# A gated cross-attention and low-rank expert layer: the first query pair is turned by blocks and DRAM instead of by TensorE, with another order in stage one and another boundary to stage two

## The chip, the cores and the metric
One core of a Trainium2 chip runs the whole kernel. The metric is the device time of one execution in microseconds (us); three runs of the kernel before gave a median of 930.25 us (928.26 to 930.46). The five engines are TensorE (PE in the profile; its weight loads are PEld), VectorE (DVE), ScalarE (ACT), GpSimd (POOL) and SyncE (SP, which only issues DMAs here). Each runs its own instructions in program order and waits on semaphores for the others.

## The reference
For each of 16 samples (x and ctx are 128 x 1024 float32), in short:
```python
qh = einsum('cn,oc->on', layernorm(x), Wq)  # 8 heads of 64 channels
kh = einsum('cn,oc->on', ctx, Wk); vh = einsum('cn,oc->on', ctx, Wv)
qh = softmax(qh, over the 64 channels of a head) * 64 ** -0.5
kh = softmax(kh, over the 1024 positions)
context = kh @ vh.T          # per head
out = context.T @ qh;  out = Wo @ out + bo
x = x + tanh(g_xattn) * out / norm(out, over channels) * g * sqrt(128)
y = layernorm(x)
scores = y @ Wr.T            # 64 experts, the top 16 are kept, softmax over them
x = x + tanh(g_ffn) * 2 * sum over k of gate[k] * (y @ A[k].T) @ B[k].T   # rank 16
```

## The kernel before
Every float32 product is made of three matmuls of rounded operands (`three_pass`, lines 59 to 63): each operand is split into a high half (a rounded copy) and a low half (what the rounding left). The high halves are mostly made by ScalarE, the low halves by VectorE or GpSimd.

**Stage one** (attention) is a software pipeline over the samples: `body(b)` of each engine works on keys and queries of sample b and finishes sample b-1, for b from 0 to 15, and a last body (16) has only the tail. TensorE multiplies keys in four blocks (`mm_k`) and queries in four pairs of position blocks (`mm_q(b, p)`, p from 0 to 3, two blocks of 128 positions and 512 channels each). VectorE takes the maxima (`max_k`, `max_q`), TensorE subtracts the query maxima (`shift_q`), ScalarE takes the exponentials (`exp_k`, `exp_q`), GpSimd adds halves of a head (`halve`), VectorE sums and inverts (`sum_q`), GpSimd scales (`normalise`). The queries then have to be turned: `tr_q` is eight TensorE transposes per pair into the PSUM tile `psT`, which has two banks shared by all transposes of keys and queries. ScalarE copies the high half from `psT` (`hi_q`), VectorE makes the low half (`lo_q`) and thereby frees the bank: `free_T` lets the next group of transposes wait for that.

Samples 1 to 14 ("turned" samples) already spare the transposes of their first key block: `exp_k(b, 0)` writes its result in an order of 32-column blocks, VectorE turns every 32x32 block in place (`turn_k`), SyncE writes the tile to DRAM and reads it back by strips (`move_k`, one DMA out and four in), ScalarE makes the high half (`hi_moved_k`) and GpSimd the low half (`lo_moved_k`).

`context` (24 matmuls, sample b-1) opens a body on TensorE, needs all low halves of the keys and gives `psX`, from which ScalarE makes `kc_hi` (`hi_kc`, line 709) and VectorE `kc_lo`; `fold` and `scale_m` make the matrix `mt`, `output` multiplies it by the turned queries, ScalarE adds the bias (`out_o`), and the result u goes to DRAM. In bodies 5 to 12 GpSimd also makes low halves of the expert weights A (`cast_a`, `lo_a`).

**The boundary.** In body 15 the work on stage two begins: the norms of samples 0 to 2 are spread over a tile (`spread` on VectorE, `spread_first`, `add_first` and `residual` on GpSimd) and added to x. SyncE loads x of sample 1 into `x_second` only when `spread_first(1)` is over (semaphore `u_done` at 2), since that tile lies over one that `spread_first(1)` reads.

**Stage two** (layer norm, routing, experts) is a loop `ffn_body`, b from 1 to 15: `up` multiplies by A in three pieces, `down(b-1)` by B. The chain of one sample is long: `sum_u` (TensorE) and `norm_u` (VectorE) give the norm, `residual` (GpSimd) x plus attention, `stats2` (VectorE) mean and deviation, `normalise` (ScalarE) y, `turn_y`, `move_y` (sixteen ScalarE copies of 32x256) and `hi_moved_y`/`lo_moved_y` turn y for `up`; `route`, `gated`, `turn_h`, `move_h`, `hi_moved_h`/`lo_moved_h` do the same for `down`.

The order of all this is written out by hand; there is no scheduler.

Of the kernel before, what the change touches and what calls it, by code (L numbers as in the profile page):

```python
# [1731 lines left out]
```

## Time and profile before
| | us |
|---|---|
| median of 3 runs | 930.25 |
| the profiled execution, its own time | 932.08 |
| its span | 930.4 |
| TensorE busy | 901.6 (97%) |
| VectorE busy | 739.7 (80%) |
| ScalarE busy | 684.3 (74%) |
| GpSimd busy | 520.0 (56%) |

The profile is of one execution. Busy time of TensorE is modelled from pipelined matmuls, so it does not show the engine at its peak, and what counts are the waits between its instructions. GpSimd's 56% is a mean over two stages: it is nearly idle in stage two.

### The profile page before, as it was taken

What the parts mean: (1) busy time and instruction counts of PE and PEld (TensorE: products, weight loads), DVE (VectorE), ACT (ScalarE), POOL (GpSimd) and SP (SyncE); (2) the same over time, 40 slices, a digit from 0 to 9 for tenths busy, and PEclk for the clock granted to TensorE, in tenths of its full rate; (3) what the DMA queues carried; (4) which work ended last, traced back from release to release, by engine and by line L of the source; (5) the groups of instructions that cost most, each with busy time, mean ns of one, the idle gap of its engine ahead of it and who ended that gap; (6) DMA issues with size and microseconds to landing.
All of it is one profiled execution on the core that took longest, in us unless ns stands there. A gap on an engine that the chain in (4) does not pass through costs nothing.

```text
span 930.4 us, 15943 instructions
## 1 busy us (share of the span) xinstructions
PE 901.6 (97%) x4732; PEld 764.7 (82%) x4732; DVE 739.7 (80%) x1523; ACT 684.3 (74%) x1400; POOL 520.0 (56%) x342
## 2 busy tenths in 40 slices
PE   7899999999999999999999999969999999999998
PEld 5687888878787787888887798869999999999896
DVE  6888889988888898898887778777777777777642
ACT  4787787777778777876876758687888888888731
POOL 3686778789778878977789856221222222222200
PEclk9999999999999999999999999979999999999999
DMA  4323423452453444233322784111111211111001
GB/s 158 114 91 125 173 103 124 161 173 100 161 182 106 146 137 159 90 137 135 119 89 87 230 329 154 46 68 68 69 69 68 69 68 68 68 68 68 23 24 46
DMA packets 35319, 104.04 MB, mean 112 GB/s; under 512 B 4432, under 2 KB 11600, under 8 KB 35280
## 3 DMA queue, kind: packets, MB, share of 16 engines
q1 hardware_dynamic: 29520, 82.59, 25.2%
q0 software_dynamic: 5472, 20.45, 6.9%
q10 hardware_dynamic: 288, 0.52, 0.2%
q8 instruction: 19, 0.31, 0.1%
q14 instruction: 20, 0.16, 0.1%
HBM read 79.43 MB, written 24.12 MB: 111 GB/s over the span
## 4 chain that ended last, share of the span: by engine, by line
PE 63%; DVE 9%; POOL 8%; issue 8%; ACT 7%; DMA 2%; SPq 0%; POOLq 0%; ACTq 0%; DVEq 0%
PE ps L61 19%; PE ps L63 18%; PE ps L62 18%; PE ps L1455 3%; PE ps L1464 3%; POOL qe L451 2%; ACT h_raw L776 2%; ACT qe L683 2%; POOL ctx_lo L410 2%; PE ps L1445 1%; DMA turn_scratch<-ek 1%; POOL qhalf L444 1%; POOL aT_lo L464 1%; ACT qT_hi L691 1%; DVE qmax L1002 1%
## 5 line engine op out<-in xcount | busy, mean ns | idle before, releaser
L522 POOL TENSOR_TENSOR rb<-u_in,rb 128x1024 f32<-128x1024 f32 x14 | 33.7, 2409 | 224.7 <-DVE rb L992 224.7
L451 POOL TENSOR_TENSOR qe<-qe,qrec 128x1024 f32<-128x1024 f32 x64 | 121.3, 1906 | 16.3 <-DVE qrec L1010 16.3
L61 PE MATMUL ps<-aT_hi,yT_hi 128*128 128x448 f32 (+2 forms) x360 | 121.1, 337 | 3.7 <-DVE yT_lo L1154 3.7
L62 PE MATMUL ps<-aT_hi,yT_lo 128*128 128x448 f32 (+2 forms) x360 | 119.7, 332 | 0.0
L63 PE MATMUL ps<-aT_lo,yT_hi 128*128 128x448 f32 (+2 forms) x360 | 119.4, 332 | 0.0
L776 ACT ACTIVATE h_raw<-hg 32x256 f32<-32x256 f32 x248 | 103.0, 415 | 16.8 <-DVE hg L1159 14.0
L444 POOL TENSOR_TENSOR qhalf<-qe 128x512 f32<-128x512 f32 x64 | 82.3, 1286 | 57.8 <-ACT qe L683 55.9
L1016 DVE TENSOR_TENSOR qT_lo<-ps,qT_hi 128x512 fp32r<-128x512 f32 x128 | 81.5, 679 | 34.7 <-ACT qT_hi L691 34.2
L776 ACT ACTIVATE y_raw<-u_in 32x256 f32<-32x256 f32 x224 | 92.9, 415 | 4.8 <-DVE u_in L1150 2.4
L61 PE MATMUL ps<-bT_hi,hT_hi 128*128 128x512 f32 x240 | 93.7, 390 | 0.3 <-DVE hT_lo L1172 0.3
L62 PE MATMUL ps<-bT_hi,hT_lo 128*128 128x512 f32 x240 | 93.5, 390 | 0.0
L63 PE MATMUL ps<-bT_lo,hT_hi 128*128 128x512 f32 x240 | 93.4, 389 | 0.0
L676 ACT ACTIVATE qe<-ps 128x1024 f32<-128x1024 f32 x48 | 49.6, 1033 | 52.9 <-PE ps L1445 52.7
L996 DVE TENSOR_REDUCE kmax<-ps 128x1 f32<-128x1024 f32 x64 | 78.0, 1219 | 10.5 <-PE ps L63 8.3
L691 ACT ACTIVATE qT_hi<-ps 128x512 fp32r<-128x512 f32 x128 | 69.5, 598 | 14.0 <-PE ps L1464 14.0
L61 PEld LDWEIGHTS ps<-aT_hi,yT_hi 128*128 128x128 f32 x360 | 69.2, 192 | 6.7 <-DVE yT_lo L1154 4.1
L668 ACT ACTIVATE ek<-ps,kmax 128x1024 f32<-128x1024 f32 x64 | 72.1, 1127 | 3.0 <-DVE kmax L996 3.0
L698 ACT ACTIVATE ekT_hi<-ps 128x512 fp32r<-128x512 f32 x100 | 54.8, 605 | 22.1 <-PE ps L1455 21.5
L62 PEld LDWEIGHTS ps<-aT_hi,yT_lo 128*128 128x128 f32 x360 | 69.3, 192 | 2.2
L63 PEld LDWEIGHTS ps<-aT_lo,yT_hi 128*128 128x128 f32 x360 | 69.1, 192 | 1.9
L1464 PE MATMUL ps<-ident,qe 128*128 128x128 f32 x512 | 67.2, 274 | 1.5 <-DVE ekT_lo L1027 1.5
L1464 PEld LDWEIGHTS ps<-ident,qe 128*128 128x128 f32 x512 | 59.2, 140 | 10.7 <-POOL qe L451 1.4
(179 smaller groups left out, 2558.8 us busy)
## 6 DMA issues: line engine op xcount, KB each, us to landing
x_in<-in_x SPq DMA_DIRECT2D x16, 512.0 KB, 3.3
ctx_in<-in_ctx SPq DMA_DIRECT2D x16, 512.0 KB, 5.4
ctxT_in<-in_ctxT SPq DMA_DIRECT2D x16, 512.0 KB, 3.3
ctxT_hi<-in_ctxT POOLq DMA_DIRECT2D x16, 512.0 KB, 4.1
u_scratch<-osb SPq DMA_DIRECT2D x16, 512.0 KB, 3.0
x<-in_x SPq DMA_DIRECT2D x15, 512.0 KB, 3.8
out<-res SPq DMA_DIRECT2D x15, 512.0 KB, 2.9
turn_scratch<-ek SPq DMA_DIRECT2D x14, 512.0 KB, 4.3
```

The lines of the kernel that those rows point to most:

```text
L61: nc.tensor.matmul(psum, whi, mhi, start=start, stop=False)
L62: nc.tensor.matmul(psum, wlo, mhi, start=False, stop=False)
L63: return nc.tensor.matmul(psum, whi, mlo, start=False, stop=stop)
L444: nc.gpsimd.tensor_tensor(qhalf[:, p % 2, :].rearrange("p (h d) -> p h d", d=DH // 2), v[:, :, 0:DH // 2], v[:, :, DH // 2:DH], ALU.add).t ...
L451: nc.gpsimd.tensor_tensor(v, v, w, ALU.mult).then_inc(q_norm, 1)
L668: nc.scalar.activation(to, of, ACT.Exp, bias=kmax[:, j:j + 1], accum_out=ksum[:, j:j + 1]).then_inc(k_exp, 1)
L691: nc.scalar.activation(qT[0][:, :, n * P:n * P + P], psT[:, h, :].rearrange("p (j n) -> p j n", n=P), ACT.Copy).then_inc(q_hi, 1)
L698: nc.scalar.activation(ekT[0][:, 4 * h:4 * h + 4, j * P:j * P + P], psT[:, h, :].rearrange("p (n d) -> p n d", d=P), ACT.Copy).then_inc(k_ ...
L776: last = nc.scalar.activation(dst[32 * q:32 * q + 32, 256 * a:256 * a + 256], src[32 * a:32 * a + 32, 256 * q:256 * q + 256], ACT.Copy)
L996: nc.vector.tensor_reduce(kmax[:, j:j + 1], psK, axis=AX.XY, op=ALU.max, negate=True).then_inc(k_max, 1)
L1016: nc.vector.tensor_tensor(qT[1][:, :, v], psT[:, h, :].rearrange("p (j n) -> p j n", n=P), qT[0][:, :, v].bitcast(f32), ALU.subtract).then ...
L1464: last = nc.tensor.transpose(psT[:, h, j * P:j * P + P], qe[:, p, w:w + P], ident[:, :])
```

## The change
Three things change together.

1. The first query pair of every sample (p = 0) is no longer transposed by TensorE. `exp_q(b, 0)` writes in 32-column blocks, `halve` and `normalise` of that pair follow that layout (the latter in two instructions), VectorE turns the blocks (`turn_q`), SyncE moves them through DRAM (`move_q`, one DMA out and four in, back into the same tile `qe`), ScalarE makes the high half in two instructions (`hi_q(b-1, 0)`, in the next body) and GpSimd the low half in two (`lo_moved_q`).
2. The order of stage one changes on all engines: on VectorE `lo_q(b-1, 1)` comes before `scale_m`, and six steps of the deviation of the next sample come after `sum_q(b, 0)`; on TensorE `shift_q(b, 1)` comes before the first half of `output`; on GpSimd `lo_a` moves to the head of the next body; on ScalarE `hi_q(b-1, 1)` comes before `exp_k(b, 1)` and `hi_moved_k` after `exp_q(b, 1)`.
3. At the boundary VectorE's `spread(1)` and GpSimd's `spread_first(1)` move to the end of body 15, and in the first bodies of stage two the norms of samples 3 and 4, the statistics of sample 3 and the routing are taken in another order; ScalarE's `square_u(4)` is split to fit, and TensorE takes `sum_u(3)` a piece earlier and `sum_u(5)` a piece later.

```diff
+        def moved_q(h):
+
+            return qe[:, 0, :].rearrange("p (a m i) -> p m a i", a=P // 32, i=32)[:, CH * h:CH * h + CH]
+
+        def turned_q(tile, h):
+
+            return tile[:, :, P * h:P * h + P].rearrange("p m (a i) -> p m a i", i=32)
...
+def move_q(b):
+
+    wait_apart(sp, sp_turns, (q_turned, b + 1))
+    sp.dma_start(turn_q_dram, qe[:, 0, :]).then_inc(q_put, 16)
+    wait_apart(sp, sp_turns, (q_put, PUT * (b + 1)))
+    for q in range(P // 32):
+        sp.dma_start(qe[32 * q:32 * q + 32, 0, :].rearrange("j (a f) -> j a f", f=256),
+                     turn_q_dram.rearrange("(a j) (q f) -> q j a f", a=P // 32, f=256)[q]).then_inc(q_moved, 16)
...
             load(x_in[:, :], x, b + 2, x_loaded)
+    if head:
+        move_q(b)
+    if ahead:
         wait_apart(sp, sp_turns, (c_lo, b + 1))
         load(ctxT_in[:, :], ctxT, b + 1, ctxT_loaded)
     if tail:
...
+    if p == 0:
+        v = qe[:, 0, :].rearrange("p (s r n i) -> p s r n i", s=2, r=2, i=32)
+        nc.gpsimd.tensor_tensor(qhalf[:, 0, :].rearrange("p (n s i) -> p s n i", s=2, i=32),
+                                v[:, :, 0], v[:, :, 1], ALU.add).then_inc(q_half, 1)
+        return
     v = qe[:, p, :].rearrange("p (h d) -> p h d", d=DH)
     nc.gpsimd.tensor_tensor(qhalf[:, p % 2, :].rearrange("p (h d) -> p h d", d=DH // 2),
                             v[:, :, 0:DH // 2], v[:, :, DH // 2:DH], ALU.add).then_inc(q_half, 1)
 
 def normalise(b, p):
     pool.wait_ge(q_rec, 4 * b + p + 1)
+    if p == 0:
+        for s in range(2):
+            v = qe[:, 0, s * HD:s * HD + HD].rearrange("p (r n i) -> p r n i", r=2, i=32)
+            w = qrec[:, 0, :].rearrange("p (n s) -> p s n", s=2)[:, s, :]
+            w = w.unsqueeze(1).unsqueeze(3).broadcast_to([P, 2, 2 * CH, 32])
+            last = nc.gpsimd.tensor_tensor(v, v, w, ALU.mult)
+        last.then_inc(q_norm, 1)
+        return
     v = qe[:, p, :].rearrange("p (h d) -> p h d", d=DH)
     w = qrec[:, p, :].unsqueeze(2).broadcast_to([P, 2 * H, DH])
     nc.gpsimd.tensor_tensor(v, v, w, ALU.mult).then_inc(q_norm, 1)
+
+def lo_moved_q(b):
+    for h in range(2):
+        pool.wait_ge(q_hi, 8 * b + h + 1)
+        nc.gpsimd.tensor_tensor(turned_q(qT[1], h), moved_q(h), turned_q(qT[0], h).bitcast(f32),
+                                ALU.subtract).then_inc(q_moved_lo, 1)
...
-def body(b, head, tail, ahead, split=False):
-    if split:
+def body(b, head, tail, ahead, low=False, cast=False):
+    if low:
+        lo_a(b - SPLIT - 1)
+    if cast:
         cast_a(b - SPLIT)
     if tail:
         halve(b - 1, 3)
-    if head:
+    if head and not started(b):
         lo_xn(b, 1)
     if tail:
+        lo_moved_q(b - 1)
         normalise(b - 1, 2)
+    if head:
+        halve(b, 0)
+    if tail:
         normalise(b - 1, 3)
-    if head:
-        halve(b, 0)
-    if head and not ahead:
-        spread_first(0)
     if tail:
         pool.wait_ge(m_hi, b)
         nc.gpsimd.tensor_tensor(mts[1][:, :, :], mt[:, :, :], mts[0][:, :, :].bitcast(f32),
                                 ALU.subtract).then_inc(m_lo, 1)
-    if split:
-        lo_a(b - SPLIT)
-    if head and turned(b):
-        lo_moved_k(b)
+    if head and started(b):
+        lo_xn(b, 1)
     if head and not ahead:
-        add_first(0)
+        spread_first(0)
     if head:
         normalise(b, 0)
         hi_c(b)
+        if turned(b):
+            lo_moved_k(b)
     if head and not ahead:
         for t in range(3):
             hi_a(t)
+        add_first(0)
     if ahead:
         lo_ctx(b + 1, 0)
         lo_ctx(b + 1, 1)
     if head:
         halve(b, 1)
         lo_c(b)
-    if head and not ahead:
-        spread_first(1)
     if head:
...
     if head and not ahead:
+        spread_first(1)
         add_first(1)
...
-        act.wait_ge(q_T, 8 * b + 2 * p - 6)
+    if started(b) and p == 0:
+        act.wait_ge(q_moved_lo, 2 * b)
+    elif started(b):
+        act.wait_ge(q_T, 6 * b - 6 + 2 * p)
...
+        act.wait_ge(q_moved, MOVED * (b + 1))
+        for h in range(2):
+            nc.scalar.activation(turned_q(qT[0], h), moved_q(h), ACT.Copy).then_inc(q_hi, 1)
+        return
...
     if tail:
+        hi_q(b - 1, 0)
         hi_kc(b - 1)
...
         exp_q(b, 0)
+        if tail:
+            hi_q(b - 1, 1)
         exp_k(b, 1)
     if tail:
-        if head:
-            hi_q(b - 1, 1)
         hi_m(b - 1)
         if not head:
...
     if head and turned(b):
-        hi_moved_k(b)
         hi_q(b - 1, 2)
     elif head:
         hi_k(b, 0)
     if head:
         exp_k(b, 2)
         exp_q(b, 1)
+    if head and turned(b):
+        hi_moved_k(b)
     if tail and head and not turned(b):
         hi_q(b - 1, 2)
     if ahead:
...
+def turn_q(b):
+    dve.wait_ge(q_norm, 4 * b + 1)
+    nc.vector.transpose(qe[:, 0, :], qe[:, 0, :]).then_inc(q_turned, 1)
...
-    if tail and head:
+    if tail and ahead:
         sum_q(b - 1, 3)
...
         max_k(b, 1)
     if last:
+        sum_q(b - 1, 3)
+    if last:
         dve.wait_ge(ctx_lo, 2 * NB)
         spread(0, rb_first[0], n_newton, 4 * NEWTON)
-    if ahead and started(b):
-        std(b + 1, range(3, NCH + 1))
     if tail and not head:
         lo_y(0)
         lo_q(b - 1, 1)
+    if tail and head:
+        lo_q(b - 1, 1)
     if tail:
         scale_m(b - 1)
-    if tail and head:
-        lo_q(b - 1, 1)
     if tail and not head:
         stats2(1, 1)
         lo_q(b - 1, 2)
-    if head and turned(b):
-        max_k(b, 2)
-        max_q(b, 1)
-    elif head:
+    if head:
         max_q(b, 1)
         max_k(b, 2)
+    if head and not turned(b):
         lo_k(b, 0)
     if not started(b):
         std(b + 1, range(5, NCH + 1))
     if head:
         sum_q(b, 0)
+    if ahead and started(b):
+        std(b + 1, range(3, NCH + 1))
     if tail and head:
         lo_q(b - 1, 2)
-    if last:
-        dve.wait_ge(xn_lo, 2 * NB)
-        spread(1, rb_first[1], n_newton, 4 * NEWTON)
     if head:
         max_k(b, 3)
         max_q(b, 2)
+        turn_q(b)
         lo_k(b, 1)
...
         std2(0, range(4, NCH + 1))
-    if head:
-        lo_q(b, 0)
+        dve.wait_ge(xn_lo, 2 * NB)
+        spread(1, rb_first[1], n_newton, 4 * NEWTON)
...
+norm_steps(3, range(7))
...
     if first:
         lo_moved_h(0)
         turn_y(2, 0)
+        norm_steps(3, range(7, NRT))
         for n in range(3, TOP):
             route_step(1, n)
+        spread_u(3)
     elif second:
+        result(0, 0, 0, 0)
+        part_u(4)
+        for n in range(3):
+            route_step(2, n)
+        lo_moved_h(1)
         turn_y(3, 1)
-        route(2)
         norm_u(4)
+        for n in range(3, TOP):
+            route_step(2, n)
     else:
         result(b - 2, (j + 1) % 2, (j + 3) % SLOTS, 2 * i + (j - 1) // 2)
+        if third:
+            part_u(5)
         lo_moved_h(b - 1)
-        if norms:
+        if norms and not third:
             part_u(b + 2)
         if ahead:
             turn_y(b + 1, j % 2)
...
             norm_u(b + 2)
     for p in range(len(PIECES)):
         gated(b, p)
+    if first:
+        lo_moved_y(2)
     turn_h(b)
-    if ahead:
+    if ahead and not first:
         lo_moved_y(b + 1)
-    if first:
-        norm_u(3)
-        result(0, 0, 0, 0)
-        part_u(4)
-        lo_moved_h(1)
...
+    if head and turned(b):
+        shift_q(b, 1)
     if tail and head:
         output(b - 1, 0, range(CH // 2))
-    if head:
+    if head and not turned(b):
...
     if head:
-        tr_q(b, 0, next(turn))
         shift_q(b, 3)
...
-    late = isinstance(i, int) and b <= 2
+    late = isinstance(i, int) and 2 <= b <= 3
```

VectorE in a body of stage one, from the last maxima before the turn to the low halves after it. Before (`kmax` and `qmax` are `max_k(b, 3)` and `max_q(b, 2)`, `ekT_lo` is `lo_k(b, 1)`, `qT_lo` is `lo_q`):
```order
L1044 TENSOR_TENSOR mt<-ps,krec 64x512 x2
L1014 ISA
L1016 TENSOR_TENSOR qT_lo<-ps,qT_hi 128x4x128
...
L996 TENSOR_REDUCE kmax<-ps 128x1
L1002 TENSOR_REDUCE qmax<-ps 128x16
L1025 ISA
L1027 TENSOR_TENSOR ekT_lo<-ps,ekT_hi 128x4x128
```
And now:
```order
L1082 TENSOR_TENSOR qT_lo<-ps,qT_hi 128x4x128
L1110 TENSOR_TENSOR mt<-ps,krec 64x512 x2
...
L1058 TENSOR_REDUCE kmax<-ps 128x1
L1064 TENSOR_REDUCE qmax<-ps 128x16
L1076 STREAM_TRANSPOSE qe<-qe 128x1024
L1091 ISA
L1093 TENSOR_TENSOR ekT_lo<-ps,ekT_hi 128x4x128
```
`lo_q(b-1, 1)` moved ahead of `scale_m` (`mt`), and the turn of the query pair stands between the maxima and `lo_k(b, 1)`.

SyncE from the loads at the boundary on. Before (`x_second` is x of sample 1, the next store is `store_u(14)`):
```order
L281 DMA x_0_105<-in_x 128x1024
L281 DMA u_first<-u_scratch 128x1024
L281 DMA x_second<-in_x 128x1024
L285 DMA u_scratch<-osb 128x1024
L281 DMA u_in_103<-u_scratch 128x1024
```
And now:
```order
L291 DMA x_0_105<-in_x 128x1024
L291 DMA u_first<-u_scratch 128x1024
L291 DMA x_second<-in_x 128x1024
L329 DMA turn_q_scratch<-qe 128x1024
L332 DMA qe<-turn_q_scratch 32x4x256 x4
L295 DMA u_scratch<-osb 128x1024
```
The move of the last sample's query pair stands behind the load of `x_second`.

GpSimd at the same place, now (`qhalf` is `halve(15, 2)`, then `spread_first(1)`, `add_first(1)`, `halve(15, 3)`):
```order
L513 DMA aT_hi<-in_AT 128x1088 x5
L471 TENSOR_TENSOR qhalf<-qe 128x512
L547 TENSOR_TENSOR u_first<-u_first,rb_first_101 128x1024
L557 TENSOR_TENSOR x_1_106<-x_second,u_first 128x1024
L471 TENSOR_TENSOR qhalf<-qe 128x512
```
Before, `spread_first(1)` stood between `lo_c(15)` and `normalise(15, 1)`, ahead of the five casts of A.

## Rows read from the trace of the kernel before

**Rows 1.** The page's first line.
```profile
span 930.4 us, 15943 instructions
```

**Rows 2.** Timeline of ScalarE (start, length, engine, line, operation): `hi_kc`, one per sample.
```profile
44.88 0.60 ACT L709 ACTIVATE kc_hi<-ps 128x512 fp32r<-128x512 f32 x1 [1.07 <-PE ps L63]
...
498.16 0.60 ACT L709 ACTIVATE kc_hi<-ps 128x512 fp32r<-128x512 f32 x1
...
533.40 0.60 ACT L709 ACTIVATE kc_hi<-ps 128x512 fp32r<-128x512 f32 x1 [0.17 <-PE ps L63]
```

**Rows 3.** Timeline of TensorE's weight loads, one sample of stage one.
```profile
353.45 1.01 PEld L1464 LDWEIGHTS ps<-ident,qe 128*128 128x128 f32 x8
...
355.71 0.19 PEld L61 LDWEIGHTS ps<-ctx_hi,wk_hi 128*128 128x128 f32 x1 [0.70 <-POOL ctx_lo L410]
...
362.21 1.02 PEld L1464 LDWEIGHTS ps<-ident,qe 128*128 128x128 f32 x8
363.49 0.19 PEld L61 LDWEIGHTS ps<-ekT_hi,ctxT_hi 128*128 128x128 f32 x1 [0.26 <-ACT osb L726]
```

**Rows 4.** Timeline of VectorE, the same sample.
```profile
333.37 1.19 DVE L1021 STREAM_TRANSPOSE ek<-ek 128x1024 f32<-128x1024 f32 x1
...
340.62 0.27 DVE L82 TENSOR_SCALAR std_t<-rstd,std_h 128x1 f32<-128x1 f32 x1
...
342.44 1.41 DVE L1044 TENSOR_TENSOR mt<-ps,krec 64x512 f32<-64x512 f32 x2
...
351.17 1.23 DVE L1002 TENSOR_REDUCE qmax<-ps 128x16 fp32r<-128x1024 f32 x1 [0.22 <-PE ps L63]
352.32 1.28 DVE L1027 TENSOR_TENSOR ekT_lo<-ps,ekT_hi 128x512 fp32r<-128x512 f32 x2
...
361.47 1.28 DVE L1027 TENSOR_TENSOR ekT_lo<-ps,ekT_hi 128x512 fp32r<-128x512 f32 x2
```

**Rows 5.** Timeline of ScalarE, the same sample.
```profile
340.19 1.03 ACT L676 ACTIVATE qe<-ps 128x1024 f32<-128x1024 f32 x1 [2.84 <-PE ps L1445]
...
342.20 1.09 ACT L691 ACTIVATE qT_hi<-ps 128x512 fp32r<-128x512 f32 x2
```

**Rows 6.** Busy time by stretch: PE, PEld, DVE, ACT, POOL, clock, DMA share, GB/s.
```profile
343.50:376.00 32.50, 32.16 (x172) 26.11 (x171) 28.10 (x49) 24.55 (x51) 27.01 (x18) 1.00 0.38 130
```

**Rows 7.** Groups by form: a low half by GpSimd from SBUF in blocks of 32.
```profile
L436 POOL TENSOR_TENSOR ekT_lo<-osb,ekT_hi 128x1024 fp32r<-128x1024 f32 x14 | 33.5, 2396 | 0.0
```

**Rows 8.** Timeline of SyncE at the end of stage one.
```profile
522.35 0.33 SPq L281 DMA_DIRECT2D x_second<-in_x  x1
```

**Rows 9.** Timeline of GpSimd, the same stretch.
```profile
519.94 2.38 POOL L506 TENSOR_TENSOR u_first<-u_first,rb_first 128x1024 f32<-128x1024 f32 x1
```

**Rows 10.** Timeline of VectorE, the same stretch.
```profile
528.45 0.21 DVE L1073 TENSOR_SCALAR nb<-mv,y 128x1 f32<-128x1 f32 x1
```

**Rows 11.** Chain that ended last (start, length, what): the key's way through DRAM.
```profile
269.52 6.39 DMA turn_scratch<-ek
277.32 2.87 DMA osb<-turn_scratch
```

**Rows 12.** The page's DMA issues: the key tile's way out (KB, us to landing).
```profile
turn_scratch<-ek SPq DMA_DIRECT2D x14, 512.0 KB, 4.3
```

**Rows 13.** Timeline of TensorE's matmuls at the start of stage two.
```profile
607.66 0.74 PE L61 MATMUL ps<-aT_hi,yT_hi 128*128 128x448 f32 x1 [3.67 <-DVE yT_lo L1154]
...
618.94 0.64 PE L1520 MATMUL ps<-part,sel 128*128 128x32 f32 x2 [4.62 <-DVE part L1190]
...
619.86 0.52 PE L62 MATMUL ps<-aT_hi,yT_lo 128*128 128x384 f32 x1
...
624.34 0.45 PE L61 MATMUL ps<-aT_hi,yT_hi 128*128 128x384 f32 x1
...
625.87 0.33 PE L63 MATMUL ps<-aT_lo,yT_hi 128*128 128x384 f32 x1
```

**Rows 14.** Timeline of ScalarE, the same stretch.
```profile
594.58 1.24 ACT L761 ACTIVATE u_in<-x,nb,y 128x1024 f32<-128x1024 f32 x1 [5.31 <-DVE nb L1073]
```

More of the change, by code:

```diff
@@ L589, in _ @@
             pool.sem_inc(a_low, 1)
-            with pool.Fori(SPLIT, SPLIT + DC) as b:
-                body(b, head=True, tail=True, ahead=True, split=True)
-            with pool.Fori(SPLIT + DC, NB - 2) as b:
-                body(b, head=True, tail=True, ahead=True)
+            body(SPLIT, head=True, tail=True, ahead=True, cast=True)
+            with pool.Fori(SPLIT + 1, SPLIT + DC) as b:
+                body(b, head=True, tail=True, ahead=True, low=True, cast=True)
+            body(SPLIT + DC, head=True, tail=True, ahead=True, low=True)
             body(NB - 2, head=True, tail=True, ahead=True)
@@ L884, in body @@
                     out_o(b - 1, 1, early)
-                if head:
-                    hi_q(b, 0)
                 if head and not ahead:
@@ L910, in ffn_body @@
                 hi_moved_h(b - 1)
+                if isinstance(i, int) and b == 2:
+                    exp_scores(2)
                 if not isinstance(i, int) or b <= NB - 2:
                     normalise(b + 1, (j + 2) % SLOTS)
-                exp_scores(b)
+                if isinstance(i, int) and b == 2:
+                    square_u(4, 0, 2, (1,))
+                else:
+                    exp_scores(b)
                 if not isinstance(i, int) or b <= NB - 2:
@@ L916, in ffn_body @@
                     hi_moved_y(b + 1)
+                if isinstance(i, int) and b == 1:
+                    square_u(4, 0, 2, (0,))
                 move_h(b)
-                if not isinstance(i, int) or b <= NB - 4:
+                if not isinstance(i, int) or 2 <= b <= NB - 4:
                     square_u(b + 3, j % 2, 2 * i + (j + 4) // 2)
@@ L1191, in part_u, with norm_steps, spread_u @@
                                         op=ALU.add, apply_transpose=True).then_inc(n_part, 1)
-            def norm_u(e):
-                before = NRT * (e - EARLY)
-                for k in range(NRT):
-                    norm_step(k, e - EARLY + 2, psN.unsqueeze(1), 1, before)
-                dve.wait_ge(x2_done, e)
-                spread(0, rb, n_step, before + NRT)
+            def norm_steps(e, steps):
+                for k in steps:
+                    norm_step(k, e - EARLY + 2, psN.unsqueeze(1), 1, NRT * (e - EARLY))
+            def spread_u(e):
+                dve.wait_ge(x2_done, e)
+                spread(0, rb, n_step, NRT * (e - EARLY + 1))
+            def norm_u(e):
+                norm_steps(e, range(NRT))
+                spread_u(e)
             stats(0)
@@ L1332, in _ @@
             turn_h(0)
+            part_u(EARLY)
             lo_b(0)
             lo_b(1)
-            part_u(EARLY)
             std2(2, range(NCH + 1))
@@ L1346, in ffn_body @@
                 second = isinstance(i, int) and b == 2
+                third = isinstance(i, int) and b == 3
                 if first:
@@ L1543, in up @@
                 elif p == 2:
[L1544 removed]
+                    pe.wait_ge(q_lo, 6 * NB)
                 first, width = PIECES[p]
@@ L1576, in body @@
                          + [("k", b, 0)] * (head and not turned(b)) + [("q", b - 1, 2)] * tail + [("k", b, 1)] * head
-                         + [("q", b - 1, 3)] * tail + [("k", b, 2), ("k", b, 3), ("q", b, 0)] * head)
-                first = ("q", b - 1, 0) if tail else None
+                         + [("q", b - 1, 3)] * tail + [("k", b, 2), ("k", b, 3)] * head)
+                first = ("k", b - 1, 3) if tail else None
                 turn = iter([first] + order[:-1])
@@ L1631, in body @@
                 if tail and head:
-                    output(b - 1, 0, range(CH // 2, CH))
+                    output(b - 1, 0, range(CH // 2, CH if ahead else CH - 1))
                 if head:
@@ L1636, in body @@
                     tr_q(b - 1, 3, next(turn))
+                if tail and not ahead:
+                    output(b - 1, 0, range(CH - 1, CH))
                 if ahead:
```

42 lines of the change are left out of this document (25 added, 17 removed).

## The prediction
> **What bounds the kernel now.** I read the page's first line [rows 1] and the table of busy times first. TensorE is busy for 97% of the span, so a microsecond counts only if TensorE's own work shrinks or one of its waits does. Then I took ScalarE's timeline for the marker `hi_kc`, one per sample, directly behind `context` [rows 2]: fourteen periods lie between 44.88 and 498.16, so a turned body lasts 453.28 / 14 = 32.38 us, and the last body with a head lasts 35.24 us. Then I read one turned body on TensorE's weight loads, on VectorE and on ScalarE [rows 3 to 5], its busy times [rows 6] and the price of the like of the new low half [rows 7], the end of stage one and the way through DRAM [rows 8 to 12], and the start of stage two [rows 13, 14]. The reader is to see three things. Inside a body TensorE hardly waits: the largest wait is 0.70 us, for GpSimd's `ctx_lo`. VectorE works in one unbroken train from 342.44 to 353.60, with stops of 0.2 to 0.3 us. At the start of stage two TensorE stands still for 3.67 and 4.62 us, and after each wait it runs at the lower of its two clock levels.
>
> **Part 1: eight transposes less.** The group `tr_q(b, 0)` loads from 362.21, and the next `context` from 363.49 [rows 3], a price of 1.28 us per body. All of it would be gain if nothing else were late. But `context` also needs `lo_k(b, 3)`, which ends at 361.47 + 1.28 = 362.75 [rows 4]. Without the transposes `context` can start at 362.8 at the earliest, so 0.7 us can be had, not 1.28.
>
> **Part 2: what VectorE gets in its place.** Per body it loses two halves of `lo_q(b, 0)`, 1.2 us that stood where it had time, and gains `turn_q`, a transpose of the form of `turn_k`, which takes 1.19 us and blocks the engine for 1.11 [rows 4]. It is put in the train, ahead of `lo_k(b, 1)`, and this is the step on which my forecast rests. I lay out the new train in the times of the body shown. `exp_q(b, 0)` starts at 340.19 as before, since nothing ahead of it changes; ScalarE is free at about 341.15 for `hi_q(b-1, 1)`, whose two halves took 1.09 us together [rows 5], so its first half is ready at about 341.75. VectorE is free at 340.62 [rows 4]; before, it used this time for six steps of the deviation and `nbias`, 342.44 - 340.62 = 1.82 us. Now `lo_q(b-1, 1)` is next and it idles till 341.8, and the 1.82 us come later, inside the train. From there everything is queued back to back, for the inputs are ready in time. The train before took 353.60 - 342.44 = 11.16 us, with some 0.55 us of short stops, so 10.6 us of work. Now it is 341.8 + 10.6 + 1.82 + 1.11 = 355.3 when `lo_k(b, 1)` ends, against 353.60.
>
> Who waits for it: `tr_q(b-1, 3)` uses the banks that `lo_k(b, 1)` frees, one half after the other. TensorE reached it at 353.45 [rows 3], and VectorE ended 0.15 us after that, with the second half needed only 0.5 us later; so the cover was some 0.4 us. Now the first half can start at 354.7 and the second at 355.35; the group ends at 355.9 instead of 354.5. Queued behind it are `mm_k(b+1, 0)`, `tr_k(b, 2)`, half an `output`, `mm_q(b, 3)` and `tr_k(b, 3)`. The wait of 0.70 us for `ctx_lo` before 355.71 [rows 3] is then covered. So `mm_k(b+1, 0)` (1.36 us) ends at 357.2 instead of 356.3, everything up to `lo_k(b, 3)` is 0.9 us later, and the next `context` starts at 362.75 + 0.9 + 0.05 = 363.7 against 363.49. The 0.7 us of part 1 are eaten, and the body takes 32.52 + 0.2 = 32.7 us. The same chain holds in bodies that were shorter before, because it goes by VectorE and not by what GpSimd did. Fourteen bodies: 14 x (32.7 - 32.38) = **+4.5 us**. The ends for a body are 31.2 (the train has slack I don't see, and only the end of `lo_k(b, 3)` counts: 32.38 - 0.7 and the wait for `ctx_lo` gone, 0.5) and 33.0. Last body with a head: the transposes go, and the stop at the turn comes in: **-1.2 us**.
>
> **Part 3: GpSimd.** It is busy for 27.01 of 32.50 us in a body with `lo_a` [rows 6]. `lo_moved_q` adds two instructions of 128 x 512 in blocks of 32; the like of 128 x 1024 took 2.40 us [rows 7], so 2.4 to 2.6 us, and `normalise(b, 0)` in two perhaps 0.1. That makes 29.7 of 32.7 us. `lo_a` moves into the wait for `exp_q(b-1, 3)` at the body's head, so what stands before `ctx_lo` grows and shrinks by the same 2.5 us. I cost it at nothing; if the cover were gone, each body would have GpSimd's 30 us and its two waits of 1 to 2 us as its length, which is the upper end of 33.0. The move through DRAM takes 6.39 us out and 2.87 us back in its slow case [rows 11]. It starts after `turn_q` at about 354.2 and is back at 364, and `hi_q` asks for it about 4 us after that: hidden.
>
> **Part 4: the last sample's move.** Here the same way is not hidden. SyncE issues in order, and `move_q(15)` stands behind the load of `x_second`, which waits for `spread_first(1)`. Before, that was over by 519.94 + 2.4 and the load was issued at 522.35 [rows 8, 9]. Now its `spread(1)` is VectorE's last work in body 15: after the last `nbias` of the statistics at 528.45 [rows 10], so 528.6 to 529.8; `spread_first(1)` runs from 530.0 to 532.4. SyncE issues `x_second` (0.33) and then the DMA out at about 532.8. With 4.3 us (the median for the key tile [rows 12]) to 6.39 us out and 2.87 us back [rows 11] plus the issues, the pair lands at 540.5 to 543. On ScalarE `hi_q(15, 0)` stands ahead of `hi_kc(15)`: `kc_hi` at 541.8 instead of 533.40 [rows 2], and behind it wait `lo_kc`, `fold` and, all of TensorE. **+8.2 us** (6 to 11). After such a wait the clock is low again: the fifteen matmuls from 619.86 to 624.34 stood 0.32 us apart, the eight after them 0.19 [rows 13], 2 us lost; **+2.0 us**. The Trainium skill ("TensorE: Matmul & The Clock Gate", What's actually happening) says that the array's clock goes between 1.2 and 2.4 GHz with recent activity, which agrees with these two spacings; without that rule the sum would be 2 us lower.
>
> **Part 5: stage two.** TensorE waited 3.67 us for y of sample 3 [rows 13], because `stats2(3)` came last in the first body and ScalarE sat 5.31 us until `nb` [rows 14]. Now the norm of sample 3 is ready before, `residual(3)` follows, and `nb` is some 6 us earlier: by the same chain (`normalise` 1.2, `turn_y` 1.2, sixteen copies 6.8, high 1.1, low 1.2) y is there at about the time that TensorE asks. The wait of 4.62 us for the partial sums of sample 5 goes because `sum_u(5)` is asked for 4 us later and `part_u(5)` comes before `lo_moved_h(2)`. The two waits are 8.3 us and the low clock behind them cost 2.2 after the second (above) and by my estimate 1.5 after the shorter first. What is late next: `lo_moved_y(2)` now stands behind `spread_u(3)` and beside GpSimd's `residual(3)`, 0.8 us, and `sum_u(4)`, `y(3)` half a microsecond each; I leave 2 us. **-10.0 us** (-5 to -12).
>
> **Sum.** The span was 930.4 and the execution 932.08, 1.8 above the median of 930.25. 4.5 - 1.2 + 8.2 + 2.0 - 10.0 = +3.5: a span of 933.9, an execution of 935.6, and 933.8 beside the median.
>
> **The rivals.**
> A. *TensorE stays the bound in stage one.* If the train has room (stops that I take for work, or `max_k(b, 3)` early enough), a body falls to 31.2 us: -16.5 instead of +4.5, so 912.8. For it speaks that VectorE is busy only 80%; against it, the gapless train of rows 4 and a cover of 0.4 us.
> B. *The last move is not waited for*, since the load of `x_second` is passed earlier than I think. Then parts of 8.2 and 2.0 fall away: 923.6. Against it: the order of SyncE and GpSimd shown with the change.
> C. *Stage two keeps its waits* in another place, since eleven steps of the norm, `result` and `part_u` are only shuffled on an engine that is nearly full there. Then -10 becomes -1: 942.8, slower. It decides where `y(3)` comes more than 3 us after 604.
> D. *The change's gain is as drawn*: A and B at once, 902.6.
>
> **How the numbers follow.** Forecast 0.56, A 0.16, B 0.14, C 0.10, D 0.04. A measurement of this kernel tells 0.3%, that is 2.8 us, from no change. The forecast's own range is 928 to 939; within it faster 0.05, same 0.20, slower 0.31, since 933.8 lies just over the line of 933.0. A, B and D are faster (0.34), C is slower. Together faster 0.39, same 0.20, slower 0.41. The range of eight in ten is 912 to 942: it takes in A and B and leaves out D and most of C.
>
> **What would show it.** Right: VectorE without a gap from about 11 us after the start of `context` to the end of `lo_k(b, 1)` 24.3 us after it; TensorE idle for 1.2 us before `tr_q(b-1, 3)`, released by `ekT_lo`; `hi_kc` 32.7 us apart; the last `hi_kc` 8 us late behind a DMA of `qe`, with a low clock after it; no wait over 1 us where stage two begins. Wrong: `hi_kc` closer than 32 us (A), `fold(15)` less than 2 us after its transposes (B), a wait over 3 us for `yT_lo` or `part` (C).

## The result, and the profile after

| | before | changed | forecast |
|---|---|---|---|
| median (lowest to highest), us | 930.36 (928.26 to 930.64) | 954.03 (952.59 to 956.08) | 933.8 (912 to 942) |
| ratio, 95% interval | | 1.0261 [1.0237, 1.0285] | |

The change makes the kernel 2.6% slower, and the time lies 12 us above my range. The profiled execution has a span of 952.3 us against 930.4 [rows 1]. The profiled execution before was itself 1.8 us above its median, and this one is at its median, so differences of spans below can come out up to 1.8 us smaller than those of medians.

The marker `hi_kc` of [rows 2] on ScalarE, with the row ahead of the last one:

```profile
44.23 0.60 ACT L762 ACTIVATE kc_hi<-ps 128x512 fp32r<-128x512 f32 x1 [1.90 <-PE ps L63]
...
501.48 0.72 ACT L762 ACTIVATE kc_hi<-ps 128x512 fp32r<-128x512 f32 x1
...
546.59 1.15 ACT L739 ACTIVATE qT_hi<-qe 128x512 fp32r<-128x512 f32 x2 [10.30 <-DMA qe<-turn_q_scratch]
547.64 0.58 ACT L762 ACTIVATE kc_hi<-ps 128x512 fp32r<-128x512 f32 x1
```

Cut at these markers, the 21.9 us by which the span grew are:

| stretch | before | changed | difference | forecast |
|---|---|---|---|---|
| start to first `hi_kc` | 44.88 | 44.23 | -0.7 | 0 |
| fourteen bodies | 453.28 | 457.25 | +4.0 | +4.5 |
| last body with a head | 35.24 | 46.16 | +10.9 | +7.0 (8.2 - 1.2) |
| last `hi_kc` to the end | 397.0 | 404.7 | +7.7 | -8.0 (2.0 - 10.0) |

The fourteen bodies went as drawn. The last line is the failure: 15.7 us of the error of 18.4 in the span. TensorE's waits from 530 us on (engine, tile, line, who released it: us in total, times, longest), which answer to [rows 13]:

```profile
PE ps L61 <- DVE kc_lo L1098: 10.6, 1, 10.6
PE ps L61 <- DVE hT_lo L1238: 8.4, 1, 8.4
PE ps L1601 <- DVE part L1256: 4.9, 1, 4.9
PE ps L61 <- DVE ekT_lo L1093: 0.9, 1, 0.9
PE ps L1613 <- ACT qe L731: 0.3, 1, 0.3
PE ps L61 <- DVE yT_lo L1220: 0.3, 1, 0.3
```

The wait for y of sample 3, 3.67 us before, is 0.3. The wait for `part` is still there, one body later (at 663.14, for `sum_u(6)`). A wait of 8.4 us for `hT_lo` (the low half that `lo_moved_h(0)` makes) before `down(0)` is new. VectorE's timeline says where it comes from:

```profile
583.10 0.18 DVE L1031 TENSOR_SCALAR ns<-ps 128x32 f32<-128x32 f32 x1
583.32 1.58 DVE L67 TENSOR_SCALAR nr<-ns 128x32 int32<-128x32 int32 x1
584.93 2.27 DVE L1035 TENSOR_TENSOR nt<-nr,ns 128x32 f32<-128x32 f32 x1
587.23 2.26 DVE L1037 SCALAR_TENSOR_TENSOR nt<-nt,nr 128x32 f32<-128x32 f32 x1
589.52 2.27 DVE L1039 SCALAR_TENSOR_TENSOR nr<-nt,nr 128x32 f32<-128x32 f32 x1
591.82 0.19 DVE L1035 TENSOR_TENSOR nt<-nr,ns 128x32 f32<-128x32 f32 x1
592.05 0.19 DVE L1037 SCALAR_TENSOR_TENSOR nt<-nt,nr 128x32 f32<-128x32 f32 x1
592.16 1.22 DVE L1238 TENSOR_TENSOR hT_lo<-h_raw,hT_hi 128x1024 fp32r<-128x1024 f32 x1
```

These are the seven norm steps that the change puts ahead of `lo_moved_h(0)`. Four of them take 1.58 to 2.27 us and three 0.18 or 0.19, for the same 32 columns. The busy time hides the cause, because these rows are counted as work. GpSimd's timeline beside them:

```profile
575.94 15.80 POOL L522 TENSOR_TENSOR bT_lo<-b_raw,bT_hi 128x1024 fp32r<-128x1024 f32 x6 [1.94 <-DMA bT_hi<-in_BT]
```

It ends at 591.74, and from 591.82 the steps are short. While it runs, the four long steps take about one GpSimd instruction each (15.80 / 6 = 2.6 us).

### The profile page after: what moved, and what is told of

Read it like the earlier page. It is cut to its first block, busy times and chain, and to the rows that moved or that the text cites. A ratio compares the mean times of both kernels' runs of the same rounds, so it can differ in the third digit from the quotient of the medians.

```text
span 952.3 us, 15772 instructions
## 1 busy us (share of the span) xinstructions
PE 892.8 (94%) x4604; PEld 751.7 (79%) x4604; DVE 746.4 (78%) x1507; ACT 684.3 (72%) x1400; POOL 563.2 (59%) x390
## 4 chain that ended last, share of the span: by engine, by line
PE 55%; DVE 22%; issue 9%; ACT 6%; POOL 4%; DMA 2%; DVEq 0%; ACTq 0%; SPq 0%; POOLq 0%
PE ps L61 17%; PE ps L62 17%; PE ps L63 17%; DVE qmax L1064 3%; DVE ekT_lo L1093 3%; DVE kmax L1058 3%; DVE qT_lo L1082 2%; ACT h_raw L831 2%; PE ps L1544 2%; PE ps L1535 1%; DVE mt L1110 1%; DVE std_t L82 1%; DVE qsum L1069 1%; DVE rstd L84 1%; PE ps L1525 1%
## 5 line engine op out<-in xcount | busy, mean ns | idle before, releaser
L486 POOL TENSOR_TENSOR qe<-qe,qrec 128x1024 f32<-128x1024 f32 x48 | 91.4, 1905 | 10.7 <-DVE qrec L1072 10.7
L1082 DVE TENSOR_TENSOR qT_lo<-ps,qT_hi 128x512 fp32r<-128x512 f32 x96 | 61.5, 682 | 26.7 <-ACT qT_hi L744 26.7
L744 ACT ACTIVATE qT_hi<-ps 128x512 fp32r<-128x512 f32 x96 | 53.5, 598 | 30.6 <-PE ps L1544 30.6
L471 POOL TENSOR_TENSOR qhalf<-qe 128x512 f32<-128x512 f32 x48 | 61.8, 1288 | 19.9 <-ACT qe L731 19.7
L1544 PE MATMUL ps<-ident,qe 128*128 128x128 f32 x384 | 52.7, 277 | 14.2 <-DVE ekT_lo L1093 14.2
L751 ACT ACTIVATE ekT_hi<-ps 128x512 fp32r<-128x512 f32 x100 | 54.4, 601 | 15.8 <-PE ps L1535 15.8
L1544 PEld LDWEIGHTS ps<-ident,qe 128*128 128x128 f32 x384 | 43.3, 140 | 26.3 <-DVE ekT_lo L1093 17.7
```

The source lines that it names most:

```text
L471: nc.gpsimd.tensor_tensor(qhalf[:, p % 2, :].rearrange("p (h d) -> p h d", d=DH // 2), v[:, :, 0:DH // 2], v[:, :, DH // 2:DH], ALU.add).t ...
L744: nc.scalar.activation(qT[0][:, :, n * P:n * P + P], psT[:, h, :].rearrange("p (j n) -> p j n", n=P), ACT.Copy).then_inc(q_hi, 1)
L751: nc.scalar.activation(ekT[0][:, 4 * h:4 * h + 4, j * P:j * P + P], psT[:, h, :].rearrange("p (n d) -> p n d", d=P), ACT.Copy).then_inc(k_ ...
L1082: nc.vector.tensor_tensor(qT[1][:, :, v], psT[:, h, :].rearrange("p (j n) -> p j n", n=P), qT[0][:, :, v].bitcast(f32), ALU.subtract).then ...
L1544: last = nc.tensor.transpose(psT[:, h, j * P:j * P + P], qe[:, p, w:w + P], ident[:, :])
```

## The experiments

Every kernel is the changed one with one edit, unless it says otherwise. The kernel before took 931.3, 929.8 and 930.5 us beside the three groups of four in which they ran (`move_first`, `hlo_first`, `turn_behind`, `old_stage_two`; `spread_early`, `spread_move`, `pool_waits`, `turn_std`; the other four). The changed kernel was not run again with them, so a gain against its 954.03 us carries an uncertainty of about 1 us.

**1. The last move first.** On SyncE:

```diff
+            move_q(NB - 1)
             sp.wait_ge(u_done, 2)
             load(x_second[:, :], x, 1, xr_loaded[1])
-            body(NB - 1, head=True, tail=True, ahead=False)
+            body(NB - 1, head=False, tail=True, ahead=False)
```

> SyncE issues the last query pair's move (to DRAM and back) before it waits for u_done 2 and loads x_second; nothing else changes against the changed kernel. Theory 1 (queue order): in the changed kernel DVE had turned the pair at 520.2 us but SyncE stood at the wait until 535.46, so with the move first it is through by about 530, the fold is released by ACT alone and the last kc_hi comes near 537.5 instead of 547.64; PE's 10.6 us wait falls to 1 to 3 us and the clock is not lowered there. 954.0 becomes 943 (941 to 945). Rival (the DRAM trip itself is slow in this stretch because weights are being loaded): the trip still lands near 545 and the time stays at 952 to 954.

Measured 950.24 us, 1.0200 [1.0183, 1.0217]. `hi_kc(15)` comes at 538.43 and the fold waits 0.98 us, as the theory says, but only 3.8 us of the expected 11 arrive, since another wait takes over. The first matmul of `up(0, 0)`, and on GpSimd the wait that it goes back to:

```profile
549.01 0.74 PE L61 MATMUL ps<-aT_hi,yT_hi 128*128 128x448 f32 x1 [7.52 <-DVE yT_lo L1212]
```

```profile
533.47 2.41 POOL L548 TENSOR_TENSOR u_first<-u_first,rb_first 128x1024 f32<-128x1024 f32 x1 [0.37 <-DVE rb_first L1055]
543.26 2.34 POOL L558 TENSOR_TENSOR x<-x_second,u_first 128x1024 f32<-128x1024 f32 x1 [7.39 <-DMA x_second<-in_x]
```

`spread_first(1)` is as late as before the edit, so `x_second` is asked for at 535.90, and `add_first(1)` holds up GpSimd. `halve(15, 3)` stands behind it, and VectorE, which has `sum_q(15, 3)` ahead of `lo_y(0)`, waits for that:

```profile
546.84 0.69 DVE L1070 TENSOR_REDUCE qsum<-qhalf 128x16 f32<-128x512 f32 x1 [7.11 <-POOL qhalf L472]
```

I had named `spread_first(1)` in my prediction as what SyncE waits for, and had not followed it to `add_first(1)`.

**2. The spread early again**, as in the kernel before; then this and edit 1 together. The same lines are taken out at their later places:

```diff
+                if last:                                 # VectorE, ahead of max_k(b, 3)
+                    dve.wait_ge(xn_lo, 2 * NB)
+                    spread(1, rb_first[1], n_newton, 4 * NEWTON)
...
                     lo_c(b)                              # GpSimd
+                if head and not ahead:
+                    spread_first(1)
```

> spread_first(1) on GpSimd and the spread of rb_first1 on VectorE stand again where the kernel before has them (behind lo_c(15) and ahead of max_k(15,3)); nothing else changes against the changed kernel. With the move alone put first, the fold's wait of 10.6 us fell to 1.0 but a wait of 7.5 us for yT_lo came, since x_second was loaded from 535.90 and GpSimd's add_first(1) and what stands behind it waited for it until 543.26. Theory 1b (the late spread_first(1) is the cause of both): u_done 2 comes near 526, x_second and the move go out at 526 and are in by 534 and 538, the last kc_hi comes at about 538 instead of 547.64 and no wait for yT_lo follows; with the 1.4 us of low clock gone 954.0 becomes 943 (941 to 945). Rival (DRAM trips in this stretch are slow, 7 us out and 5 back, whoever issues them when): kc_hi near 542 and 946 to 949.

> The same as spread_early, and SyncE moves the last query pair before it waits for u_done 2. Theory 1b: the move is hidden altogether (in by 536), kc_hi near 537.5 behind ACT's last exponentials, x_second is issued at 529 and in by 537, so yT_lo comes just in time: 942 to 943, at most 1 us below spread_early. Rival (x_second is what counts): slower than spread_early by 2 to 4, with a wait for yT_lo before up(0,0).

Measured 951.4 us, 1.0229 [1.0212, 1.0246], and 942.14 us, 1.0130 [1.0113, 1.0147]. Alone it gives 2.6, with the move first 11.9. The first kernel lies outside both ranges: `hi_kc(15)` comes only at 545.26, later even than its rival put it. DRAM trips are slow in this kernel, but not whoever issues them when, as the rival has it; the second kernel's are not. What each DMA of the way back took to land, in `spread_early`, then in the changed kernel:

```profile
L332 SPq DMA_DIRECT2D qe<-turn_q_scratch x4: 326/459/731, 532.8 to 534.4; - x4
...
DMA to landing us min/median/max: 7.5/7.7/9.8
```

```profile
L332 SPq DMA_DIRECT2D qe<-turn_q_scratch x4: 326/425/432, 542.4 to 543.7; - x4
...
DMA to landing us min/median/max: 2.5/2.8/2.9
```

And the busy share of the DMA engines in `spread_early` (last column but one):

```profile
524.00:528.00 4.00, 4.00 (x25) 3.43 (x24) 3.75 (x12) 2.03 (x5) 4.00 (x3) 1.00 0.01 3
528.00:532.00 4.00, 3.12 (x15) 2.28 (x14) 3.82 (x10) 1.69 (x3) 4.00 (x7) 1.00 0.98 297
532.00:536.00 4.00, 4.00 (x20) 3.24 (x18) 0.96 (x3) 3.95 (x16) 3.27 (x2) 1.00 1.08 375
536.00:540.00 4.00, 2.27 (x18) 1.73 (x16) 0.00 (x0) 0.56 (x3) 1.28 (x1) 1.00 1.06 338
```

GpSimd issues five loads of `aT_hi`, 544 KB each, from 528.9 on. What SyncE issues from 532.8 is behind them in time. It does not wait for `x_second`, which landed 4.2 us after its issue at 527.12, before the way back was asked for. In `move_first` the way back went out from 528.46, when the loads began (529.04), and its four DMAs took 2.6 to 7.6 us. In `spread_move` it goes out from 527.08, ahead of them, takes 2.6 to 3.2 us, and TensorE hardly waits: 0.2 us before the fold and 0.3 for `yT_lo`. So two causes cover one another, the order on SyncE and the late `spread_first(1)`: alone each edit shows a third of what the two give together, or less. That the burst of weights is the third is read from these traces; no run moves the loads.

**3. `hT_lo` ahead of the seven steps:**

```diff
-            norm_steps(3, range(7))
...
                     lo_moved_h(0)
                     turn_y(2, 0)
-                    norm_steps(3, range(7, NRT))
+                    norm_steps(3, range(NRT))
```

> The seven first steps of norm_steps(3) stand behind lo_moved_h(0) and turn_y(2,0) instead of ahead of them; nothing else changes against the changed kernel. Theory 2 (the seven small steps wait one by one for GpSimd's bT_lo instructions, and hT_lo stands behind them): hT_lo starts at about 583 and takes one GpSimd instruction more than its 1.2 us (2.4 us), down(0) starts at about 585.7 instead of 593.43 with no low clock in it; a wait of 2 to 3 us for yT_lo before up(2) comes in its place since gated(1) is late, so the time falls by 6 to 8: 947 (945 to 949). Rival (hT_lo is late because of ACT or of memory traffic): down(0) stays near 593 and the time stays within 2 us of 954.

Measured 949.46 us, 1.0190 [1.0173, 1.0207], so -4.6 where -7 was expected, and 0.5 above the range. `down(0)` starts at 586.19 after a wait of 1.0 us; `hT_lo` takes 2.83. But the steps still stand beside GpSimd, `gated(1)` and `lo_moved_y(2)` behind them are late, and 4.39 us of wait for `yT_lo` come before `up(2, 0)`, where I expected 2 to 3.

**4. GpSimd waits for the steps:**

```diff
+            pool.wait_ge(n_step, 7)
             for k in range(KC):
                 if by_pool(k):
                     lo_b(k)
```

> GpSimd waits for the seventh step of norm_steps(3) before its first bT_lo instruction; nothing else changes against the changed kernel. Theory 2 (a VectorE instruction with both inputs in SBUF waits for the end of GpSimd's running tensor_tensor): with GpSimd idle all seven steps take 0.15 to 0.25 us each, lo_b(0) and lo_b(1) take 1.2 us each instead of 4.53 for the two, hT_lo is ready 3 us or more before PE's down(0) could start; down(0) starts near 584 instead of 593.43 but waits inside for bT_lo (GpSimd works from about 580 on, six by 2.5 us), and ends near 600 instead of 606.7: 947 (944 to 951). Rival (the steps are slow for another reason, such as waits between neighbours): they still take 2.3 us each.

Measured 951.0 us, 1.0223 [1.0206, 1.0240], the upper end of the range expected. The time is 3.0 lower, not 7, since `down(0)` then waits for `bT_lo` inside (3.0 us in three waits), but the question was the length of the steps. VectorE here:

```profile
580.79 0.18 DVE L67 TENSOR_SCALAR nr<-ns 128x32 int32<-128x32 int32 x1
581.01 0.19 DVE L1036 TENSOR_TENSOR nt<-nr,ns 128x32 f32<-128x32 f32 x1
581.24 0.19 DVE L1038 SCALAR_TENSOR_TENSOR nt<-nt,nr 128x32 f32<-128x32 f32 x1
581.47 0.19 DVE L1040 SCALAR_TENSOR_TENSOR nr<-nt,nr 128x32 f32<-128x32 f32 x1
...
582.47 3.21 DVE L1239 TENSOR_TENSOR hT_lo<-h_raw,hT_hi 128x1024 fp32r<-128x1024 f32 x1 [0.36 <-ACT hT_hi L858]
```

The same four instructions, 0.18 to 0.19 us each with GpSimd idle. GpSimd starts at 582.20, and now `hT_lo` pays, 3.21 us for work of 1.22. This shows that the steps are long because GpSimd's instructions run beside them. The Trainium skill ("SBUF — State Buffer", SBUF: two separate sides) says that GpSimd and some VectorE operations, those with two inputs in SBUF among them, share one port pair that whoever starts first holds for its whole instruction; the trace agrees, with 2.27 us for an instruction of 0.19.

**5. The second stage by itself**, from both sides: the changed kernel with the second stage of the kernel before (`ffn_body` of VectorE and ScalarE, VectorE's lines ahead of it and TensorE's `late`), and the kernel before with that of the changed one, of which these are the core:

```diff
-                late = isinstance(i, int) and b <= 2
+                late = isinstance(i, int) and 2 <= b <= 3
...
+            norm_steps(3, range(7))
```

> Stage one and the boundary as in the changed kernel, the second stage in the order of the kernel before. From the last kc_hi (547.64) to the end the kernel before took 397.0 us, the changed one 404.7. Theory 2 (the new order of stage two costs 8 by itself): 547.6 + 397 + 1.5 for the low clock at the start = 946.5 (944 to 949), with hT_lo blocked once (2.4 us) and no wait of 8 us before down(0). Rival (stage two is slow because of what stage one leaves it, GpSimd being later against VectorE): down(0) waits 5 us or more with the old order too, and the time is 951 to 956.

> The kernel before with the changed kernel's order of the second stage and nothing else of the change. Theory 2 (the seven norm steps wait for GpSimd's bT_lo one by one and hold hT_lo): down(0) waits 7 to 9 us for hT_lo, the wait of 3.67 us for yT_lo goes, the one of 4.6 us for part stands one body later, and the time from the last kc_hi to the end is 402 to 405 us instead of 397.0: 936 to 939 beside about 930. The prediction's reading (the new order takes both waits away): 920 to 925.

Measured 946.32 us, 1.0161 [1.0144, 1.0178], as theory 2 put it, and 936.48 us, 1.0059 [1.0044, 1.0073], the low end of what it put. From the last `hi_kc` the first takes 943.6 - 546.45 = 397.1 us, the second 934.8 - 533.18 = 401.6. So the old order takes 397 us behind either stage one, and the new one costs 4.6 us of span behind the old stage one (6.0 by the medians) and 7.6 behind the new one. TensorE's waits in the kernel before with only this part:

```profile
PE ps L61 <- DVE hT_lo L1181: 8.5, 1, 8.5
PE ps L1545 <- DVE part L1199: 4.2, 1, 4.2
```

**6. The turn behind `lo_k(b, 1)`**, and then also the last std steps where the kernel before has them:

```diff
-                    turn_q(b)
                     lo_k(b, 1)
+                    turn_q(b)
```

> DVE turns the query pair behind lo_k(b,1) instead of ahead of it; nothing else changes against the changed kernel. Theory 3 (the row of VectorE work ahead of lo_k(b,1) is what lengthens a body): lo_k(b,1) is 1.1 us earlier, the waits of 0.92 and 1.25 us for ekT_lo before tr_q(b-1,3) go, the turn fills an idle stretch of 0.8, and a body is 0.7 to 1.0 us shorter: 31.8 instead of 32.66, 954.0 becomes 942 (940 to 945). Rival (the body is bound by TensorE or by another chain, the waits come back elsewhere): body within 0.2 of 32.66, 951 to 955.

> turn_q behind lo_k(b,1) as in turn_behind (942.7, body 31.95 us), and besides the last std steps (1.8 us) stand where the kernel before has them, ahead of lo_q(b-1,1), where VectorE idles 1.04 us for qT_hi. Theory 3: PE was busy 438.6 of 446.5 us in turn_behind, so at most 0.5 us a body is left; the steps fill the idle stretch and lo_k(b,1) comes 1 us earlier still: body 31.6 to 31.9, time 938 to 942. Rival (mt is now late, by 0.8 us, and the fold and m chain with it): body 32.0 to 32.3, 943 to 948.

Measured 942.74 us, 1.0120 [1.0103, 1.0137], and 951.02 us, 1.0236 [1.0213, 1.0259]. Bodies last (491.74 - 44.49) / 14 = 31.95 us and (498.75 - 43.71) / 14 = 32.50. One line moved by one place gives 11.3 us. The second kernel's body lies above its rival's 32.3, and its time, 3 us above the rival's range: all waits for `ekT_lo` ahead of `tr_q(b-1, 3)` are gone there too, but `lo_q(b-1, 1)`, `mt` and `qmax` of `max_q(b, 1)` stand behind the std steps, `shift_q(b, 1)` starts 0.4 us later in the body, and the `output` behind it 0.5:

```profile
346.01 0.70 PE L1525 MATMUL ps<-qmax,ident_r 128*128 128x512 f32 x2 [0.17 <-DVE qmax L1064]
```

The stretch in which VectorE idles 1.04 us was not free to fill: what it waits for there is on TensorE's path as well.

**7. `sum_u` behind `up(b, 1)` in every body from 2 on:**

```diff
-                late = isinstance(i, int) and 2 <= b <= 3
+                late = not isinstance(i, int) or b >= 2
```

> sum_u stands behind up(b,1) in every body from b = 2 on, not only in 2 and 3; nothing else changes against the changed kernel. Theory 4 (the wait of 4.95 us for part belongs to the first body whose sum stands ahead of up(b,1), while usq of that body is made behind move_h; in the bodies of the loop the sum has 4 us more anyway): the wait at 663 goes, nothing replaces it, 954.0 becomes 947.5 to 950 (the low clock after it goes too). Rival (it only moves to the next body or comes back as a wait for hg or yT_lo): 952 to 955.

Measured 946.19 us, 1.0169 [1.0154, 1.0183]; 1.3 us below the range expected. The wait of 4.95 us is 0.64, nothing takes its place, and the granted clock behind it is 1.00 (662 to 667 us), where it was 0.50 in the changed kernel (663 to 668).

**8. All of it together:** edits 1 and 2, the turn behind `lo_k(b, 1)` and the old stage two; then `late = True` besides.

> The turn of the query pair with its three costs taken away: turn_q behind lo_k(b,1); spread_first(1) and its spread as in the kernel before with the last move put first on SyncE; the second stage in the order of the kernel before. By the profiles of the single edits: kc_hi of body 14 at 491.7 (turn_behind), 37.2 to the last one (spread_move), 397.1 to the end (old_stage_two), 1.7 around: 927.7 (925 to 930) beside 930.4 for the kernel before, a ratio of 0.997. Rival (the gains overlap or the turn pays nothing against the kernel before): 930 to 935.

> best_turn, and sum_u behind up(b,1) in every body. By theory 4 the wait of 3.7 us for part goes with the low clock behind it: 4 to 6 us below best_turn, 922 to 924. Rival (the wait comes back elsewhere): within 1 us of best_turn.

Measured 925.39 us, 0.9950 [0.9938, 0.9962], and 919.97 us, 0.9884 [0.9869, 0.9898]. Both beat the kernel before, by 0.5% and 1.2%. The second is 2 us below the range expected, since the first was already 2 below the middle of its own; the 5.4 between them are as expected. The bodies of the first last (491.01 - 43.77) / 14 = 31.95 us against 32.38 before, so the turned query pair is worth 6 us once nothing else pays for it. TensorE's largest waits after 500 us in the faster one:

```profile
PE ps L61 <- DVE yT_lo L1215: 3.8, 1, 3.8
PE ps L1512 <- DVE qmax L1059: 1.2, 1, 1.2
```

## Why the prediction was wrong

Part 5 failed. I wrote that in stage two both waits go with their low clocks, and left 2 us for what is late next: -10.0. By itself the part costs +4.6 (experiment 5), since a new wait of 8.4 us for `hT_lo` comes in and the wait for `part` stays. With the stop at the boundary ahead of it the stretch costs 7.7, of which 1.4 lie before `turn_h(0)`, where I had put 2.0 of low clock (the granted clock is 0.50 from 549.0 to 553.5).

- The first half was wrong, though the 3.67 us for `yT_lo` went. I had `nb` of sample 3 some 6 us earlier. Before and now:

```profile
594.33 0.22 DVE L1073 TENSOR_SCALAR nb<-mv,y 128x1 f32<-128x1 f32 x1
```

```profile
609.75 0.21 DVE L1139 TENSOR_SCALAR nb<-mv,y 128x1 f32<-128x1 f32 x1
630.03 0.47 PE L61 MATMUL ps<-aT_hi,yT_hi 128*128 128x448 f32 x1 [0.28 <-DVE yT_lo L1220]
```

  Counted from the last `hi_kc`, `nb` comes after 62.1 us where it came after 60.9, and TensorE asks for y(3) after 82.1 where it asked after 70.6 [rows 13]. The wait is gone because TensorE is 11.5 us later. With `hT_lo` first (experiment 3) `nb` comes after 59.7: in no kernel with the new order was it more than 1.2 us earlier. In `pool_waits`, where TensorE asks for y(3) after 78.6, 1.59 us of the wait are back. So no run shows that the new order takes this wait away, and that it went is luck.
- What I costed at nothing was the place of the seven steps that were to bring `nb` forward. The sum has no term for them, and I did not ask who else ran at the time. Moving them behind `hT_lo` takes its wait from 8.4 to 1.0 us. The trace of the kernel before shows such rows: `hT_lo` took 2.45 us beside GpSimd's six `bT_lo` and 1.23 a sample later, and a `gsel` of 64 columns took 2.30. I did not read them.

```profile
567.16 2.45 DVE L1172 TENSOR_TENSOR hT_lo<-h_raw,hT_hi 128x1024 fp32r<-128x1024 f32 x1 [1.82 <-ACT hT_hi L802]
572.04 2.30 DVE L1110 TENSOR_TENSOR gsel<-gsel,ex 128x64 f32<-128x64 f32 x1
589.37 1.23 DVE L1172 TENSOR_TENSOR hT_lo<-h_raw,hT_hi 128x1024 fp32r<-128x1024 f32 x1 [0.81 <-ACT hT_hi L802]
```

- The second half was wrong as a mechanism. `sum_u(5)` was given more time, so `sum_u(6)` is the first that stands early, and waits 4.95 us. The wait belongs to the border between the late and the early order, not to sample 5 (experiment 7).

The other steps:

- Parts 1 and 2 were right in place, cause and size: 457.25 / 14 = 32.66 us a body against 32.7. `tr_q(b-1, 3)` is released by `ekT_lo`, and putting the turn one place later gives the body back (31.95).

```profile
355.61 0.42 PEld L1544 LDWEIGHTS ps<-ident,qe 128*128 128x128 f32 x4 [1.32 <-DVE ekT_lo L1093]
```

```profile
342.64 1.29 DVE L1082 TENSOR_TENSOR qT_lo<-ps,qT_hi 128x512 fp32r<-128x512 f32 x2 [1.04 <-ACT qT_hi L744]
353.75 1.23 DVE L1076 STREAM_TRANSPOSE qe<-qe 128x1024 f32<-128x1024 f32 x1
354.91 1.25 DVE L1093 TENSOR_TENSOR ekT_lo<-ps,ekT_hi 128x512 fp32r<-128x512 f32 x2
```

  VectorE's train is the one of [rows 4], with the idle time that I forecast at its head.
- Part 3 was right: GpSimd is busy for 29.8 of 32.5 us (343.5 to 376), as forecast, and in `turn_behind` the body falls to 31.95 with the same work on it, so the additions are hidden. The same engine was where part 5 broke.
- Part 4 was right in mechanism and 3.9 us small in size. Counted from `hi_kc(14)`, the DMA out was issued after 34.4 us (535.90 - 501.48) where I had 34.6 (532.8 - 498.16). Then it took 6.5 us out and 4.2 back until ScalarE went on, so `hi_kc(15)` came after 46.2 and not 43.6. Another 0.2 is a slip of mine: 541.8 - 533.40 is 8.4, not the 8.2 of the sum. The other 1.2 us I had taken off for the missing transposes of this body, which are worth nothing where the move sets the end. SyncE's timeline:

```profile
535.46 0.33 SPq L291 DMA_DIRECT2D x_second<-in_x  x1
535.90 0.36 SPq L329 DMA_DIRECT2D turn_q_scratch<-qe  x1
542.37 1.75 SPq L332 DMA_DIRECT2D qe<-turn_q_scratch  x4
```

- Rival C, stage two keeping its waits, had the right side and the right place, and both its signs came (y(3) late, a wait over 3 us for `part`). Its price was 9 where 14.6 was measured, and its mechanism, a full VectorE, was not the one found. I gave it 0.10.

What stays open: 1.7 of the 3.1 us by which the changed kernel's stage two (404.7) is slower than the same order in the kernel before (401.6) are not explained by the 1.4 of low clock. Of them 0.7 are the longer wait for `part` (4.95 against 4.21); the rest was not followed. The wait of 3.8 us for `yT_lo` in the fastest kernel was left as it is.

## What to carry to other kernels

- Before you move a small instruction on VectorE, look at what GpSimd does at its new time, and compare rows of the same form in both places: an instruction of 0.19 us cost 2.3 here. A longer row of the same form can hide a wait that no list of waits shows.
- When an order is changed by hand for the first bodies of a loop, look for the wait at the border to the next one before you book it as gone.
- When a wait has gone, compare the time at which its input is ready, not only the wait: here it went because TensorE came later.
- A stop with several causes gives little when one is taken away. Test them together before you drop a theory: 3.8 and 2.6 us alone were 11.9 together.
